# A graph attention kernel with its layer sweeps and preparations written out instead of looped

## The reference

```
h = relu(layernorm(x))
e = (h @ Ws) @ (h @ Wt).T                       # layer 0
x = x + softmax(where(adj > 0, e, -9e15)) @ (h @ Wc)
h = relu(layernorm(x))
Wh = h @ W                                      # layer 1
e = leaky_relu((Wh @ a1)[:, None] + (Wh @ a2)[None, :], 0.2)
x = x + elu(softmax(where(adj > 0, e, -9e15)) @ Wh)
```

## Time and profile before

| | |
|---|---|
| median of 3 runs | 1520.61 us (1518.73 to 1529.33) |
| profiled execution | 1534.86 us, span 1533.0 us |
| preparation for layer 0 | up to about 95 us |
| layer 0, 64 tiles | about 95 to 1000 us |
| preparation for layer 1 | about 1008 to 1070 us |
| layer 1, 64 tiles | about 1075 to 1525 us |

### The profile page before, as it was taken

How to read it: one execution, slowest core, us unless ns; L and a number is a source line. 1 busy time by engine, 2 the same in 40 slices (tenths; PEclk the granted TensorE clock), 3 DMA queues, 4 the chain that set the end, 5 groups by cost and what they waited for, 6 DMA issues and landing times.

```text
span 1533.0 us, 78545 instructions
## 1 busy us (share of the span) xinstructions
PE 1311.9 (86%) x31947; PEld 1143.1 (75%) x31947; DVE 1272.6 (83%) x2313; ACT 1043.3 (68%) x2064; POOL 1.5 (0%) x11
## 2 busy tenths in 40 slices
PE   1836879999999999999999898867899988988986
PEld 1625767887878888888888787754788878877986
DVE  5777779999989999999999898436798978977977
ACT  1835556667666777767666676467788877877975
POOL 0000000000000000000000000000000000000000
PEclk9977899999999999999999999989899999999999
DMA  7039879999999999999999998410333323323322
GB/s 228 0 154 341 284 267 367 360 370 369 363 363 359 386 365 375 370 377 369 378 364 363 356 346 306 128 31 0 92 100 113 113 72 100 112 72 100 113 72 79
DMA packets 114304, 363.21 MB, mean 237 GB/s; under 512 B 11504, under 2 KB 44528, under 8 KB 81392
## 3 DMA queue, kind: packets, MB, share of 16 engines
q1 hardware_dynamic: 114160, 361.02, 66.4%
HBM read 319.03 MB, written 41.94 MB: 235 GB/s over the span
## 4 chain that ended last, share of the span: by engine, by line
PE 47%; DMA 18%; issue 13%; DVE 12%; ACT 6%; DVEq 1%; SPq 1%; ACTq 1%
DMA arena<-in_adjB 17%; PE ps L809 15%; PE ps L796 9%; PE ps L708 5%; DVE arena L1347 4%; PE ps L729 3%; PE ps L670 3%; PE ps L702 3%; DVE arena L1322 3%; PE ps L703 2%; PE ps L658 2%; DVE mx L1356 2%; ACT arena L1002 2%; ACT arena L905 1%; PE ps L590 1%
## 5 line engine op out<-in xcount | busy, mean ns | idle before, releaser
L1495 DVE TENSOR_SCALAR arena<-arena 128x128 f32 (+1 forms) x768 | 202.6, 340 | 63.2 <-ACT arena L1052 58.2
L729 PE MATMUL ps<-arena 128*128 128x129 f32 x2048 | 248.0, 279 | 4.6 <-issue 4.6
L809 PE MATMUL ps<-arena 128*128 128x129 f32 x2048 | 247.6, 280 | 2.2 <-issue 2.2
L729 PEld LDWEIGHTS ps<-arena 128*128 128x128 f32 x2048 | 239.6, 195 | 4.9 <-issue 4.9
L809 PEld LDWEIGHTS ps<-arena 128*128 128x128 f32 x2048 | 239.5, 195 | 2.5 <-issue 2.5
L1322 DVE TENSOR_SCALAR arena<-arena 128x2048 fp8e4<-128x2048 int32 x192 | 234.8, 1224 | 7.6 <-DMA arena<-in_adjB 1.5
L988 ACT ACTIVATE arena<-ps 128x512 f32<-128x512 f32 x256 | 153.0, 598 | 124.8 <-PE ps L670 124.8
L982 ACT ACTIVATE arena<-ps 128x512 f16<-128x512 f32 x256 | 153.9, 601 | 62.6 <-PE ps L658 62.4
L796 PE MATMUL ps<-arena 128*32 128x132 f16 x8192 | 160.7, 231 | 41.4 <-issue 29.8
L1011 ACT ACTIVATE arena<-arena 128x2048 fp8e4<-128x2048 int32 x64 | 122.3, 1911 | 103.6 <-DMA arena<-in_adjB 103.6
L1052 ACT ACTIVATE arena<-ps 128x396 f32<-128x396 f32 (+1 forms) x384 | 151.1, 463 | 59.2 <-PE ps L796 59.2
(11 more groups left out here) (166 smaller groups left out, 1469.0 us busy)
## 6 DMA issues: line engine op xcount, KB each, us to landing
arena<-in_adjB SPq DMA_DIRECT2D x256, 1024.0 KB, 7.3
sel_pick<-arena SPq DMA_DIRECT2D x64, 256.0 KB, 9.6
sel<-arena SPq DMA_DIRECT2D x64, 256.0 KB, 9.6
arena<-sel_pick SPq DMA_DIRECT2D x64, 256.0 KB, 3.4
arena<-sel SPq DMA_DIRECT2D x64, 256.0 KB, 2.7
x_t<-in_x SPq DMA_DIRECT2D x64, 64.0 KB, 8.2
x_mid<-y_t SPq DMA_DIRECT2D x64, 64.0 KB, 8.5
arena<-x_mid SPq DMA_DIRECT2D x8, 512.0 KB, 4.9
```

The costliest lines, as they stand in the source:

```text
L729: last = nc.tensor.matmul(pv_ps, p_T[:, s * P:(s + 1) * P], v_sel[:, b, s, :], start=False, stop=(s == SB - 1), skip_group_check=True)
L809: last = nc.tensor.matmul(xv_ps[b], w_msk[:, b, s, :], x1_sel[:, b, s, 0:VW], start=False, stop=(s == SB - 1), skip_group_check=True)
L1495: last = nc.vector.tensor_scalar(w_raw[b][:, k, :], own, x1_sel[:, b, k, D + 2:D + 3], x1_sel[:, b, k, D + 1:D + 2], ALU.mult, ALU.max)
```

## The change

The sweeps of layer 0 and layer 1, the preparations of modes 0 and 1 and the statistics are written out on every engine: Python loops take the place of the hardware loops, so that each step stands in the program with constants for its counts and addresses. What is computed, the order of the work on each engine and the buffers stay as they are. Only the path that isn't taken keeps its loops.

```diff
-        def tile_sweep(eng, step):
-
-            for i in range(6):
+        def tile_sweep(step):
+
+            for i in range(TILES + 4):
                 step(i, i % 2)
-            with eng.Fori(6, TILES - 3, 2) as i:
-                step(i, 0)
-                step(i + 1, 1)
-            for i in range(TILES - 2, TILES + 4):
-                step(i, i % 2)
...
-        def batch_sweep(eng, step, last):
-
-            for u in range(STEPS):
-                step(0, u)
-            with eng.Fori(1, TILES // STEPS) as j:
+        def batch_sweep(step, last):
+
+            for j in range(TILES // STEPS):
                 for u in range(STEPS):
                     step(j, u)
             last()
+
+        def group_sweep(eng, mode, step):
+
+            if mode < 2:
+                for G in range(2, PREP - 2):
+                    step(G, G % 2)
+            else:
+                with eng.Fori(2, PREP - 3, 2) as G:
+                    for b in range(2):
+                        step(G + b if b else G, b)
...
-                    with dve.Fori(2 * q, 2 * q + 2) as r:
-                        for i in range(quarter // 2):
-                            row_moments(mode, r * (quarter // 2) + i)
+                    for i in range(quarter):
+                        row_moments(mode, q * quarter + i)
```

More of the change, by code:

```diff
@@ L460, in _ @@
             sp.dma_start(w_sb[:, 0, :], W1).then_inc(w_in, 16)
-            tile_sweep(sp, tile_io)
+            tile_sweep(tile_io)
             sp.wait_ge(y_out[0], 16 * (TILES // 2))
@@ L495, in last_store @@
                     sp.wait_ge(y8_out, 16 * STEPS)
-                batch_sweep(sp, batch_io, last_store)
+                batch_sweep(batch_io, last_store)
             def layer_io(layer):
@@ L629, in prepare, with group @@
                     transpose_h(b + 2, b, mode)
[L630 to L633, removed]
+                def group(G, b):
+                    project(G, b, base, mode)
+                    transpose_h(G + 2, b, mode)
+                group_sweep(pe, mode, group)
                 project(PREP - 2, 0, base, mode)
@@ L772, in _ @@
             pe.wait_ge(proj_lo, PREP)
-            tile_sweep(pe, tile_step)
+            tile_sweep(tile_step)
             pe.wait_ge(y_ready, TILES)
@@ L829, in last @@
                                      ).then_inc(differ_ps, 1)
-                batch_sweep(pe, step, last)
+                batch_sweep(step, last)
             def row_scores(t, s, c):
@@ L972, in prepare @@
                 group(1, 1, True)
-                with act.Fori(2, PREP - 3, 2) as G:
-                    for b in range(2):
-                        group(G + b if b else G, b, True)
+                group_sweep(act, mode, lambda G, b: group(G, b, True))
                 group(PREP - 2, 0, False)
@@ L1040, in _ @@
             prepare(0)
-            tile_sweep(act, tile_step)
+            tile_sweep(tile_step)
             act.wait_ge(wT_ready, 1)
@@ L1101, in last @@
                     exp_h(STEPS - 1)
-                batch_sweep(act, step, last)
+                batch_sweep(step, last)
             def mask(tau, m):
@@ L1310, in prepare @@
                     group(b, b, True)
-                with dve.Fori(2, PREP - 3, 2) as G:
-                    for b in range(2):
-                        group(G + b if b else G, b, True)
+                group_sweep(dve, mode, lambda G, b: group(G, b, True))
                 group(PREP - 2, 0, False)
@@ L1578, in last @@
                                             ).then_inc(decided_redo, 1)
-                batch_sweep(dve, step, last)
+                batch_sweep(step, last)
             def layer_steps(layer):
@@ L1716, in _ @@
             mean_values()
-            tile_sweep(dve, tile_step)
+            tile_sweep(tile_step)
             dve.wait_ge(pos_kept, TILES)
```

## The result

The changed kernel takes 1672.72 us (median of 4 runs, 1665.21 to 1683.41) against 1524.97 us before (median of 4): a ratio of 1.099, 95% interval 1.094 to 1.105. It is slower by 148 us.

What follows compares the result with a forecast made beforehand. TensorE and the transfers were taken to bound layer 0, TensorE alone layer 1. Layer 0's +204, layer 1's -32 and -3 for preparations and statistics summed to +169 us, a median of 1690 us, range 1560 to 1775 us.

Steps and rivals of the forecast that it cites:

- What bounds it: TensorE and the transfers together bound layer 0, with VectorE close behind; TensorE alone bounds layer 1.
- Layer 0, the packets: Straight code in layer 0 fetches 2.6 instruction packets a tile, 140 in 54 tiles, 2.3 MB.
- Layer 0, the tile: A layer 0 tile takes 12.4 + 3.6 stalls + 0.7 ScalarE wait + 0.3 clock = 17.0 us, against 13.23: +204 us.
- The term of the clock: In layer 0, 0.3 us a tile for TensorE's half-speed time, a small part kept because of start-up waits.
- What a loop end is worth in layer 0: Each of 27 removed loop ends in layer 0 is worth 1.7 us, part of it due to the transfers.
- Layer 1: Batches 1 to 7 lose six loop ends: 25.6 us of stalls plus 7 of clock, -32 us, between -20 and -39.
- Preparations and statistics: Loop ends removed in both preparations and the statistics give -3 us, with 0 and -6 as ends.
- The other streams: Straight VectorE, ScalarE and SyncE need a block only every few tiles in layer 0, so nothing is charged.
- fetching is hidden: Rival: in layer 0 the sequencer stays a block ahead, tiles of 12.9 us, 1468 us in all; chance 0.10.
- the stalls are mostly absorbed: Rival: layer 0 tiles of 14.4 us as TensorE catches up while adjacency data is late, 1549 us; chance 0.10.
- The case at full load: Rival: with the whole pipeline running, layer 0 tiles take 18.8 us, 1785 us in all; chance 0.13.
- the lower and the upper bound: Layer 0's cost lies between +63 us (shortest fetched tile, 14.4 us) and +299 us (loop's first pass, mean 18.8 us).

Runs made afterwards that it cites:

- light_looped: l0_looped with only an eighth of each adjacency chunk loaded from tile 2 on: 1415.58 us, ratio 0.935.
- l0_looped: The changed kernel with layer 0's steps 6 to 61 back in the hardware loop on all engines, body of two steps: 1474.16 us, ratio 0.970.
- l1_alone: The kernel before with layer 1's batches alone written out: 1489.07 us, ratio 0.979.
- pe_straight: The changed kernel with SyncE, ScalarE and VectorE back in their layer 0 loops, TensorE alone straight there: 1673.45 us, ratio 1.101.
- pe_body4: l0_looped with four steps instead of two in TensorE's loop body, the other engines at two: 1759.93 us, ratio 1.163.

## Why the prediction was right, step by step

The forecast was 1690 us with 1560 to 1775; it came to 1673. As a change it was +169 us, and +148 was measured, in the medians and in the two profiles. The profiles split it. From the first L694 (L699) to the last, layer 0 takes 858.8 us before (104.4 to 963.2) and 1055.9 after (96.9 to 1152.8): +197, where +204 was forecast. Layer 1's seven intervals give -39 instead of -32, the preparations and statistics -11 instead of -3, and 2 us are added at the end. So the mechanism and the path were right, and three terms were each 7 or 8 us off, all to the same side. The steps:

**What bounds it.** Held. TensorE bounds layer 1, and in layer 0 TensorE and the transfers did so together: with an eighth of the load a looped tile fell from 13.23 us to 12.41 and no further.

**Layer 0, the packets.** 140 were forecast for 54 tiles, 144 came. Two slips stand beside this. The list of signs says some 20 packets in 100 us; 140 packets in 54 tiles of 17 us are 15, and 16 came. And the steps that were straight before are 0 to 5 and 62 on, not 64 on; the 54 steps are counted rightly.

**Layer 0, the tile.** Forecast 17.0 us, measured 16.90, but three of the four terms were off, and not all to the same side. The stalls were put at 3.6 us a tile and measured 164.7 / 54 = 3.05. The wait for ScalarE, 0.7 us, was kept and is gone (0.9 us in all): slow tiles leave the transfers time, and ScalarE's list has no wait for adjacency data any more, where the earlier trace rows has 82.5 us. The clock was put at 0.3 us, since I laid the 0.88 of the earlier trace rows on the start-up; in the steady part it is 0.90. TensorE's busy time a tile rose from 685.92 / 54.9 = 12.5 us (726.8 / 13.23 = 54.9 tiles) to 738.73 / 54 = 13.7. In light_looped it is 12.41 x 641.86 / 650 = 12.25 us, at a clock of 1.00:

```profile
200.00:850.00 650.00, 641.86 (x17294) 559.46 (x17400) 632.92 (x839) 482.29 (x682) 0.00 (x0) 1.00 0.29 95
```

So beside a tile without stalls, from which the sum starts, the clock costs about 1.4: 12.4 + 3.05 + 1.4 = 16.85. The term of the clock was mis-sized by a factor of more than four. The stalls and the wait were 0.55 and 0.7 us too high, the clock 1.1 too low, and that these nearly cancelled is luck.

The pauses cost twice: once as such, and once in half-speed stretches behind them. Behind the pause of 1.99 us that ends at 652.11 the changed kernel has this stretch, with a granted clock of 0.50:

```profile
652.10:654.00 1.90, 1.89 (x22) 1.69 (x23) 1.90 (x3) 0.15 (x1) 0.00 (x0) 0.50 1.05 410
```

The 32 matmuls that weigh the values take 5.06 us there, and 3.79 us in light_looped, where no pause stands ahead of them and the clock is 1.00:

```profile
652.74 5.06 PE L734 MATMUL ps<-arena 128*128 128x129 f32 x32
```

```profile
205.19 3.79 PE L744 MATMUL ps<-arena 128*128 128x129 f32 x32
```

At an eighth of the load, with short pauses, the clock is 1.00 and this part vanishes.

**What a loop end is worth in layer 0.** Wrong, though it entered the sum only as a bound. I read 1.7 us for each end from the turns of 12.4 and 14.1 us, with a part of it for the transfers. All of it was the transfers: light_looped has the same loop ends and no turns. With full load the wait of the earlier trace rows comes in about one of two tiles. That it is mostly the one with the loop end isn't fixed: in l0_looped 10 of the 27 tiles with a loop end take less than 13 us, and 9 of the 27 without one take more. What decides it wasn't tried.

**Layer 1.** Forecast -32 us, between -20 and -39. The profiles give 39, with l1_alone's too (347.0 us against 385.7), though that kernel's time fell by only 32. The removed pairs of stalls at the loop ends, and the clock back from 0.96 to 1.00, are as named; but the clock came back whole, and I had credited half of it. 25.6 + 13.5 = 39 us is what the profiles have. VectorE did not take over (TensorE is busy 97%, VectorE 94%).

**Preparations and statistics.** Forecast -3 us, with -6 as an end. The first L694 came at 104.4 us before, and the first L699 at 96.88 us in the changed kernel, 7.5 us earlier for the statistics and layer 0's preparation. Between layer 0's last prefix and layer 1's first L1534, where mode 1's preparation stands, another 4 us went (173.4 to 169.6). So this term was 11 us, beyond its end of 6. Most of the 7.5 us is in the statistics; VectorE's timeline has, before and then after:

```profile
7.83 2.02 DVE L1205 BATCH_NORM_STATS2 stat<-arena  x8 [4.12 <-DMA arena<-in_x]
```

```profile
7.38 3.19 DVE L1208 BATCH_NORM_STATS2 stat<-arena 128x6 f32<-128x128 f32 x16 [3.67 <-DMA arena<-in_x]
```

Not only the gaps at the loop ends went, which the earlier trace rows shows and I counted, but each instruction came faster: 252 ns in the loop, where registers were worked out for its addresses between two of them, and 199 ns in the straight form. 64 of them make 3.4 us.

**The other streams.** Charged at nothing, and pe_straight against the changed kernel shows it (1673.45 against 1672.72 us). Their instructions come on a second instruction queue, q14, with 24 packets in the changed kernel's layer 0 and none in pe_straight's: one in about two tiles. They do stall where VectorE is nearly full: its waits in the changed kernel's layer 1 (1270 to 1650 us) begin with

```profile
DVE arena L1495 <- issue: 17.8, 24, 2.4
```

Before the change VectorE had no such wait in layer 1 (1134 to 1471 us). TensorE is the bound there, and its waits for what comes of this are small.

**The rivals.** That fetching is hidden did not come in layer 0. It holds where the DMA engines are idle for most of the time (layer 1, and 21 us of 199 left at an eighth of the load), which is the point from which I said it would decide. That the stalls are mostly absorbed, with tiles of 14.4 us, did not come: TensorE has no other wait left that could hide them (0.9 us in all). The case at full load, tiles of 18.8 us, did not come either. By the earlier trace rows its two tiles were 14.4 and 23.1 us long, so the shortest fetched tile is one of them, and the lower and the upper bound rest on the same pair. The long one has pauses of 2.44, 4.08 and 2.41 us in straight code and none at a loop end; in the changed kernel the 54 tiles lie between 13.2 and 18.9 us, and none is like it. pe_body4, with the pauses of a loop's start added, comes near the upper bound: (1759.93 - 1474.16) / 54 = 5.3 us a tile above the looped kernel.

## What to carry to other kernels

A straight program isn't free of control cost; it trades loop ends for instruction traffic, which here came late when the data transfers were many. Look for the instruction queue in the DMA view and for "issue" pauses in runs of equal instructions: an engine that issues hundreds of instructions a tile should loop over a body that stays on the chip when DMA is busy, and the engines that issue few can be straight. A loop whose body doesn't stay is the worst of both, so count the body's instructions before unrolling it further.

## What the hardware did that I had not expected

TensorE's granted clock went with the fetch stalls in the steady state too: 0.90, 0.96 and 1.00 with 3.05, 1.6 and 0.37 us of pauses a tile. The pauses grew steadily with the load: they are already 1.6 us with the DMA engines busy for 0.63 of the time.

The instruction packets themselves did not get slower. One took 1.03, 1.07 and 1.12 us on average in layer 0 with full, half and an eighth of the adjacency, so the lateness arises before a packet starts to move. That it waits there behind the adjacency's packets is the likely reading; it was not shown directly, only that fewer bytes end it.
